# Units 0 and 1 of the shared expert as one of 512 rows; the last rows mixed in the steps and stored by tile

## What is computed

```python
def _L0_attn_ref(x, w_qkva, gamma):
    h = _rmsnorm(x, gamma)
    qkva = jnp.einsum('bnd,ed->bne', h, w_qkva)
    q, kv, a = jnp.split(qkva, 3, axis=-1)
    a = jax.nn.sigmoid(a)
    _, y = lax.associative_scan(binary_operator, (a, kv), axis=1)
    return q * y          # y_t = a_t * y_(t-1) + kv_t

def _L0_ffn_ref(x, router_w, w_gate, ...):
    logits = x_flat @ router_w.T                     # 7 experts
    top_vals, top_idx = jax.lax.top_k(logits, 2)
    routed_out = _swiglu(x_flat, w_gate, w_up, w_down)
    mixed = jnp.einsum('end,ne->nd', routed_out, combine)
    shared_out = _swiglu(x_flat, sw_gate, sw_up, sw_down)
    return mixed + jnp.mean(shared_out, axis=0)

x = x + _L0_attn_ref(_layernorm(x), ...)
x = x + _L0_ffn_ref(_layernorm(x), ...)
```

## Time and profile before

| | us |
|---|---|
| median of 3 runs | 985.65 (985.25 to 985.87) |
| the profiled execution | 986.29 |
| its span, first to last instruction | 984.5 |
| TensorE busy | 973.7 (99%) |
| VectorE busy | 587.9 (60%) |
| ScalarE busy | 477.5 (49%) |
| GpSimd busy | 396.8 (40%) |

### The profile page before, as it was taken

One profiled execution on the slowest core, in us unless ns is written; L12 is line 12 of the kernel. 1 busy time (PEld: TensorE's weight loads), 2 busy tenths in 40 slices (PEclk: granted clock), 3 DMA queues, 4 the chain that ended last, 5 costly groups with the idle time before them and its releaser, 6 DMA issues.

```text
span 984.5 us, 15882 instructions
## 1 busy us (share of the span) xinstructions
PE 973.7 (99%) x5565; PEld 849.3 (86%) x5565; DVE 587.9 (60%) x1042; ACT 477.5 (49%) x769; POOL 396.8 (40%) x265
## 2 busy tenths in 40 slices
PE   8999999999999999999999999999999999999997
PEld 6888998888889998888888888888888999999886
DVE  7988687788663134455445544654465455656576
ACT  4565434322422325446545554554455566667563
POOL 3336100000021243464645463655465588776200
PEclk9999999999999999999999999999999999999999
DMA  9433300000059995634463456355634576774393
GB/s 324 115 87 86 87 22 22 17 6 22 1 142 353 317 305 177 198 125 147 163 204 111 150 176 197 88 174 175 202 88 167 187 264 231 271 213 160 120 298 107
DMA packets 146018, 155.06 MB, mean 157 GB/s; under 512 B 75433, under 2 KB 134322, under 8 KB 138802
## 3 DMA queue, kind: packets, MB, share of 16 engines
q1 hardware_dynamic: 139232, 136.08, 42.7%
q0 software_dynamic: 6720, 18.36, 5.9%
q10 hardware_dynamic: 18, 0.01, 0.0%
HBM read 127.67 MB, written 26.74 MB: 157 GB/s over the span
## 4 chain that ended last, share of the span: by engine, by line
PE 88%; DVE 5%; DMA 2%; ACT 2%; issue 1%; SPq 1%; POOL 0%; DVEq 0%; ACTq 0%; POOLq 0%
PE ps L1150 38%; PE ps L1128 15%; PE ps L1106 11%; PE ps L1131 8%; PE ps L1012 6%; PE ps L1172 4%; PE ps L1192 3%; DMA sorted_rows<-x_stage 2%; PE ps L994 1%; PE ps L1200 1%; SPq L447 1%; ACT h_hi L878 1%; PE ps L1023 1%; DVE h_lo L1748 1%; DVE ps L1742 1%
## 5 line engine op out<-in xcount | busy, mean ns | idle before, releaser
L1150 PE MATMUL ps<-xs_hi,w_both 128*128 128x512 f32 x1216 | 380.4, 391 | 0.1
L1150 PEld LDWEIGHTS ps<-xs_hi,w_both 128*128 128x128 f32 x1216 | 228.3, 188 | 49.1 <-DVE ps L1742 1.2
L644 POOL TENSOR_TENSOR w_both<-w_raw,w_both 128x2048 fp32r<-128x2048 f32 x45 | 223.5, 4967 | 106.2 <-ACT w_both L815 97.6
L1150 PE MATMUL ps<-xs_lo,w_both 128*128 128x512 f32 x608 | 236.7, 389 | 0.0
L1128 PE MATMUL ps<-w_both,h_hi 128*128 128x512 f32 x656 | 233.0, 398 | 0.1
L1131 PE MATMUL ps<-w_both,h_lo 128*128 128x256 f32 x656 | 184.1, 281 | 0.0
L1748 DVE TENSOR_TENSOR h_lo<-ps,h_hi 128x512 fp32r<-128x512 f32 x152 | 105.2, 692 | 103.6 <-ACT h_hi L878 82.2
L668 POOL DMA_INDIRECT x_stage<-z_rows,idx_x x70 | 73.4, 1048 | 224.5 <-DVE idx_x L1661 160.9
L1742 DVE TENSOR_TENSOR ps<-ps,silu 128x512 f32<-128x512 f32 x152 | 106.3, 699 | 91.9 <-ACT silu L871 63.3
L871 ACT ACTIVATE silu<-ps 128x512 f32<-128x512 f32 x152 | 90.8, 597 | 134.0 <-PE ps L1150 133.8
L1128 PEld LDWEIGHTS ps<-w_both,h_hi 128*128 128x128 f32 x656 | 123.3, 188 | 30.2 <-DVE h_lo L1748 0.4
(11 more groups left out here) (228 smaller groups left out, 1080.8 us busy)
## 6 DMA issues: line engine op xcount, KB each, us to landing
w_raw<-in_L_ffn_w_gate_dram SPq DMA_DIRECT2D x20, 1024.0 KB, 4.9
w_raw<-in_L_ffn_w_up_dram SPq DMA_DIRECT2D x20, 1024.0 KB, 7.3
w_raw<-in_L_ffn_w_down_dram SPq DMA_DIRECT2D x20, 1024.0 KB, 6.1
sorted_rows<-x_stage SPq DMA_DIRECT2D x32, 256.0 KB, 2.2
x_rows<-sorted_rows SPq DMA_DIRECT2D x128, 64.0 KB, 2.0
w_spare<-in_L_ffn_w_up_dram SPq DMA_DIRECT2D x6, 1024.0 KB, 6.6
...
```

The lines of the kernel that those rows point to most:

```text
L644: pool.tensor_tensor(w_lo[buf][:, k, :], w_raw[buf][:, k, :], w_hi[buf][:, k, :].bitcast(F32), ALU.subtract).then_inc(wlo_ready[k], 1)
L1150: last = pe.matmul(ps[:, 2 * (j % 2) + part, :], w[:, part, kd * H + j * P:kd * H + (j + 1) * P], xx[:, h // 2, kd, :], start=i == 0, stop ...
```

## The change

Units 0 and 1 are one quad. Its x is made ready in turn 5 (unit 0) and turn 7 (unit 1), given by `UNIT_AT`; the x of units 2 and 3 is loaded ahead of the store of the last z, and made ready in its steps. The work owed is spread anew: on TensorE `last_back` ahead of block 0, the routings ahead of blocks 2, 4 and 7, `turn_last_z` ahead of block 5 (now into banks 4 and 5), `ranks` behind the third tile of the down part. On VectorE the totals and blocks of the ranks stand behind the down part, `places` in step 0 of unit 2 and `pair_targets` in its step 2. In the last quad three of four `mix_own` go into steps 2, 5 and 6, the fourth and the last batch come ahead of the adds, the last two tiles are summed in a bank each and are added and stored one by one.

```diff
-    MIXED = [2 * OWN + BATCH * (b + 1) for b in range(5)] + [4 * OWN + BATCH * 6]
...
+    OWN_TILES = (4, 4, 4, 5, 7, 8)
+    MIXED = [TOP * OWN_TILES[b] + BATCH * (b + 1) for b in range(BATCHES)]
...
+        UNIT_AT = {NC - 3: 0, NC - 1: 1}
...
+            for n in (2, 3):
+                load_x(n, n, z_dram, n % 2)
             store_z(NC - 1)
             sp.wait_ge(z_out[NC - 1], 16)
-            for n in range(2, SA):
+            for n in range(4, SA):
                 load_x(n, n, z_dram, n % 2)
...
-            store_own(2)
             sp.wait_ge(mixed, MIXED[5])
             store_tiles(5 * BATCH, 6 * BATCH)
-            store_own(3)
-            sp.wait_ge(outs, 16 * 8)
+            store_own(2)
+            for t in range(ST):
+                sp.wait_ge(last_added, t + 1)
+                store_tiles(T0 + 3 * ST + t, T0 + 3 * ST + t + 1)
+            sp.wait_ge(outs, 16 * 9)
...
-                act.activation(zT[NC - 1][:, :, :], ps[:, 0:2, :], ACT.Copy).then_inc(zT_ready, 1)
+                act.activation(zT[NC - 1][:, :, :], ps[:, 4:6, :], ACT.Copy).then_inc(zT_ready, 1)
...
                                ).then_inc(a_ready, 1)
                 if g == 0:
                     h_rows(1)
-                elif g < NC - 2:
-                    h_rows(g + 2)
+                else:
+                    if g in UNIT_AT:
+                        x_hi(UNIT_AT[g], UNIT_AT[g])
+                    if g < NC - 2:
+                        h_rows(g + 2)
                 if g + 1 < NC:
                     h_hi_part(g + 1)
-                else:
-                    x_hi(0, 0)
...
-            slot(0, 0, early=True, turns=((2, 1),), between={1: lambda: z_rows(NC - 1), 2: zT_copy})
-            slot(1, 1, early=True, turns=((1, 1), (3, 2)))
+            quad(0, 0, early=True, between={1: lambda: z_rows(NC - 1), 5: zT_copy})
...
                 pe.wait_ge(z_ready, NC)
-                pe.wait_ge(gated, 5)
+                pe.wait_ge(res_ready, NC)
...
-                        last = pe.transpose(ps[:, kd, k * P:(k + 1) * P], z[:, kd], ident[:, :])
+                        last = pe.transpose(ps[:, 4 + kd, k * P:(k + 1) * P], z[:, kd], ident[:, :])
...
+                if g in UNIT_AT:
+                    pe.wait_ge(x_split, UNIT_AT[g] + 1)
...
-                            last = pe.matmul(ps[:, 6, (t - ST) * D:(t - ST + 1) * D], a[:, j, t * P:(t + 1) * P],
+                            o = ps[:, t + 4, 0:D] if apart else ps[:, 6, (t - ST) * D:(t - ST + 1) * D]
+                            last = pe.matmul(o, a[:, j, t * P:(t + 1) * P],
                                              w[:, 2, j * D:(j + 1) * D], start=j == 0 and i == 0,
                                              stop=j == JH - 1 and i == len(terms) - 1)
-                last.then_inc(down_psum, 1)
+                    if apart:
+                        last.then_inc(last_psum, 1)
+                    if t == ST and JH + 1 in between:
+                        between[JH + 1]()
+                if not apart:
+                    last.then_inc(down_psum, 1)
...
-            slot(0, 0, 0, between={0: last_back, 2: lambda: last_routes(NC - 3),
-                                   6: lambda: last_routes(NC - 2), JH - 1: turn_last_z},
-                 down=lambda: last_routes(NC - 1), skip=0)
-            slot(1, 1, 0, between={1: ranks}, skip=0)
+            quad(0, 0, 0, skip=0, wide=False, between={
+                0: last_back, 2: lambda: last_routes(NC - 3), 4: lambda: last_routes(NC - 2), 5: turn_last_z,
+                7: lambda: last_routes(NC - 1), JH + 1: ranks})
...
-            quad(NB0 + 2, (NB0 + 2) % 4, 0, ahead=0, wide=False)
+            quad(NB0 + 2, (NB0 + 2) % 4, 0, ahead=0, wide=False, apart=True)
...
-                if g == NC - 1:
-                    turn_x(0, LD)
-                scan(g, None if g + 1 < NC else lambda: x_lo(1, 0))
+                if g in UNIT_AT:
+                    n = UNIT_AT[g]
+                    turn_x(n, LD)
+                    scan(g, lambda: x_lo(n + 1, n))
+                else:
+                    scan(g)
...
+            def add_last(t, tile):
+
+                row = resid[:, tile:tile + 1, :]
+                dve.wait_ge(last_psum, t + 1)
+                dve.wait_ge(mixed, mixes[0])
+                dve.tensor_tensor(row, ps[:, 6 + t:7 + t, 0:D], row, ALU.add).then_inc(last_added, 1)
...
+                    if ("gated", j) in between:
+                        between["gated", j]()
...
-                if shared is not None:
+                if shared is not None and apart:
+                    for t in range(ST):
+                        add_last(t, shared * ST + ST + t)
+                elif shared is not None:
                     add_narrow(n + 1, shared * ST + ST)
...
-            def kinds_and_places():
-                rank_kinds()
-                places()
...
-            slot(0, 0, turns=((1, 1, loads(1)),), shared=0, early=True, skip=0, between={
-                ("gated", 0): lambda: statistics2(NC - 1), 1: logits_and_z,
-                2: lambda: take_logits(NC - 2, 7), "down": choices})
-            slot(1, 1, turns=((0, 1, loads(2)), (2, 2, loads(3))), shared=1, early=True, skip=0, between={
-                0: rank_totals, 1: rank_blocks, 2: rank_quarters, "down": kinds_and_places})
+            def totals_and_blocks():
+                rank_totals()
+                rank_blocks()
+                rank_quarters()
 
             def ahead_of(n):
                 return ((1, 2, loads(n + 2)), (4, 3, loads(n + 3)))
 
+            quad(0, 0, turns=ahead_of(0), shared=0, early=True, skip=0, between={
+                ("gated", 0): lambda: statistics2(NC - 1), 2: logits_and_z, 5: lambda: take_logits(NC - 2, 7),
+                "down": choices, "half": totals_and_blocks})
+            rank_kinds()
...
-                2: {0: pair_targets, 3: lone_places, 6: lone_targets, 7: find_pairs, "down": move_all,
+                2: {0: places, 2: pair_targets, 3: lone_places, 6: lone_targets, 7: find_pairs,
+                    "down": move_all,
...
-            quad(NB0 + 2, (NB0 + 2) % 4, shared=SA + 2, between={
-                0: lambda: sum_weighed(2), 1: lambda: add_weighed(2),
+            quad(NB0 + 2, (NB0 + 2) % 4, shared=SA + 2, apart=True, between={
+                0: lambda: sum_weighed(2), 1: lambda: add_weighed(2), 2: lambda: mix_own(2, (0,)),
                 3: lambda: sum_weighed(3), 4: lambda: add_weighed(3),
-                7: lambda: sum_weighed(4),
-                "down": lambda: (add_weighed(4), mix_own(2, (0, 1)), mix_own(3, (0, 1))), "half": lambda: mix_weighed(5)})
+                5: lambda: mix_own(2, (1,)), 6: lambda: mix_own(3, (0,)), 7: lambda: sum_weighed(4),
+                "down": lambda: (add_weighed(4), mix_own(3, (1,)), mix_weighed(5))})
```

More of the change, by code:

```diff
@@ L1133, in down_wide, with quad @@
                 return last
-            def quad(n, h, buf, m=None, between=(), skip=NS, ahead=2, wide=True):
+            def quad(n, h, buf, m=None, between=(), skip=NS, ahead=2, wide=True, apart=False):
                 pe.wait_ge(x_split, n - skip + 2)
```

6 lines of the change are left out of this document (5 added, 1 removed).

## The result

| | before | after |
|---|---|---|
| median, in runs side by side | 985.62 (4 runs) | 993.81 (992.62 to 994.23, 4 runs) |
| ratio | | 1.0078, 95% interval 1.0066 to 1.0091 |
| span of the profiled execution | 984.5 | 992.3 |
| mean granted clock of TensorE over the span | 0.998 | 0.995 |

The forecast was 987.5, with a range up to 989.3. The time is above its end. The 0.998 of the kernel before is no loss: by quarters of a us its clock is full until 980.4 us, 1.9 us behind the last matmul, and half from there to the end, when TensorE has nothing left to do.

The account below looks back on a forecast made before the run. TensorE, busy 599.85 of 600 us from 300 to 900 us, was taken to bound the kernel; median 985.65 + 4.1 for the front - 2.3 for the end gave 987.5, range 986.0 to 989.3.

Parts of the forecast that it names:

- the clock falls in the new waits: Rival: one fall of TensorE's clock to half doubles a step of 2.72 us to 5.4, time 990.2; chance 0.10.
- The front: Everything ahead of the kernel's end, from scan to experts: +4.1 us in sum, from 3.4 to 4.9.
- The turn back: Last 512 rows: now first in the unit, it loses the 1.44 us of matmuls that covered VectorE's product: +1.45.
- Routing 6: Second routing in the unit, before block j = 4: TensorE waits for VectorE's zT, +1.9 (1.5 to 2.4).
- Routing 7: Third routing in the unit, after j = 6: TensorE waits for ScalarE's copy of zT, +0.95 (0.7 to 1.2).
- Turn 5: Unit 0 taken up here: ScalarE's xs_hi waits for VectorE's transpose, delaying h_rows and hT_lo: +0.45 (0.3 to 0.8).
- Unit two: places and pair_targets moved into its steps make a VectorE gate late for TensorE's j = 5: +0.8 (0.3 to 1.2).
- Matmuls saved: 512-row unit against two 256-row slots: gate and up matmuls -1.3, down part -0.3 (0 to -0.6).
- the switches: Going from a short transpose to a long matmul costs slightly more than to a short one: 0.15.
- The end: After the last h_lo: shorter VectorE list 1.55, stores -0.8, together -2.3 (-1.6 to -2.7).
- small stores gain nothing: Rival: DMA engines still busy with stores ahead, so the last part gives only -1.6, time 988.2; chance 0.10.

Follow-up runs that it names:

- the kernel with the end alone: The kernel before with only the end's part of the change made: 983.31, ratio 0.9977.
- the kernel with the filled waits: The changed kernel with unused 512-column matmuls: eight ahead of the last turn back, eight ahead of routing 6, four ahead of routing 7: 988.56.
- the kernel with the rest of the waits: The changed kernel with last turn back, routings, VectorE's z transpose and pair_targets later, logits of turn 6 before h_lo, ScalarE's rows ahead of xs_hi: 983.06, ratio 0.9971.

## Why the prediction was wrong, step by step

**The clock is the step that failed.** The rival "the clock falls in the new waits" had a chance of 0.10, one fall and a price of 2.7. The reason given against it was that the fall at the end of the kernel came only after TensorE had issued nothing for longer than any of these waits lasts. Read closely, that passage of the trace does not bear it out. The last matmul began at 978.24 and ended at 978.52, and the clock fell at 980.44: 1.9 us of idle time, no longer than the wait of 1.9 that I forecast and shorter than the 2.04 and 2.15 that came.

```profile
978.24 0.28 PE L1172 MATMUL ps<-w_both,h_lo 128*128 128x256 f32 x1
978.50:980.25 1.75, 0.01 (x1) 0.00 (x0) 1.65 (x2) 0.00 (x0) 0.00 (x0) 1.00 0.44 150
980.25:980.50 0.25, 0.00 (x0) 0.00 (x0) 0.19 (x1) 0.00 (x0) 0.00 (x0) 0.88 0.00 0
```

Nor is one such row a rule: in the kernel with the end alone TensorE idled from 977.67, and the clock fell only at 982.9, 5.2 us later. The row also says nothing of a wait of 2.15 that is followed by 1.7 us of matmuls with 7 columns, and I had named these tiny matmuls without drawing the conclusion. Three stretches came, 5.1 us. Filling the waits gave 5.25 back, and doubling one routing without any wait made a fall too. The size of one fall was also wrong: 1.7 and not 2.7, because it lasts 3.4 us and not the 5.4 of a whole block at half.

**The front without the clock** is 988.56 - 983.31 = +5.25, from the kernel with the filled waits and the one with the end alone; both have the end's change. Forecast +4.1, from 3.4 to 4.9, so 1.1 too little. Term by term:
- The turn back: the wait is 2.04 where before had 0.31, so +1.75; forecast +1.45. The turn back comes 0.3 later than in the sum, relative to the turn before it (10.36 against 10.06 us), and VectorE's product does not: it is done 10.00 behind that turn in both. It is the 0.3 by which TensorE takes up work later after the long wait.
- Routing 6: 2.15 against 1.9. ScalarE's z_rows (112.20, 2.08 long) did delay SiLU of block 2, as said. SiLU began at 114.19.
- Routing 7: 0.96 against 0.95. The copy of zT began at 132.54, right behind xs_hi, and lasted 1.01.
- Turn 5: from the turn back in turn 5 to that in turn 6 TensorE needs 12.42 instead of 11.80, +0.6 against 0.45. The cause I gave, ScalarE's order, is not the one that holds TensorE up: with that order put right in the kernel with the rest of the waits the turn takes 12.40. hT_lo stands behind the lo part in VectorE's scan, which I had not costed, since "the rows taken up in turn 7 are the same work" was true for turn 7 alone.
- Unit two: 0.64 against 0.8. Unit four: 0.45 before a list part, forecast 0.
- These sum to some 1.0 over the forecast (0.3 + 0.25 + 0.15 - 0.15 + 0.45).

**Matmuls saved** can be read in the kernel with the rest of the waits, from the start of block 0 to the narrow tiles of unit two: 170.44 - 100.74 = 69.7, of which 0.52 is the wait in unit two, against 170.59 - 99.95 = 70.6 in before, of which 0.31 is the wait for y_sb. So 1.15 less, where the forecast has 1.6 less and 0.15 for the switches, 1.45. That is another 0.3 over it. A block behind a piece put between blocks starts some 0.1 slower (0.31 from its first matmul to its second, where 0.23 is usual). The front's terms together come to 1.3 over the forecast. In the kernel with the filled waits the 0.3 of the later start is gone, so there they come to 1.0, against 1.1 measured.

**The end**: -2.5 against -2.3. The store is worth 0.65 of it, forecast 0.8, and by the reason that the prediction gave: the store of 512 KB is no longer just ahead. The small size adds 0.1, which can't be told from nothing. The rival "small stores gain nothing" is true of the size and false of the end (1.6 was its number). The Trainium skill (DMA: Bandwidth & Descriptors, Rules for kernel authors) would have the tiles coalesced; here 128 KB or 256 KB makes no difference that I can measure (983.31 against 983.44).

**Sum**: forecast +1.8. Add 5.1 for the clock, 1.3 for the front, and take 0.2 for the end: +8.0. Measured +8.2.

What stays open: why a given wait of 2 us is followed by a fall in one run and not in another. The wait for y_sb had none in the profiled run of the kernel after and one in two others. The length of the idle time does not decide it: behind the last matmul of the kernel, with nothing to do in each, the clock fell after 1.9 us in one profiled execution and after 5.2 in another. I have no experiment that fixes this.

The best kernel here, 983.06, and the end alone on the old front, 983.31, cannot be told apart. So the unit of 512 rows, even with the large waits gone, gives back most of the 1.15 that its matmuls save: 0.6 in turn 5 (12.40 against 11.80) and 0.52 in the wait of unit two.
